# Mixer slots in a new order: gate passes first on VectorE, small multiplies moved to ScalarE

## The reference

```python
proj = jnp.einsum('bsd,ed->bse', x, in_proj_w)
gate = proj[..., :INTER]
hBC  = proj[..., INTER:INTER + CONV_DIM]
...
hBC = jax.nn.silu(conv(hBC) + conv_b)        # depthwise, 4 taps along the sequence
hs, Bm, Cm = ...                             # 128 heads of 64, 8 groups of 128
xch = (hs * dt[..., None])
Y_diag = jnp.einsum('bzlhn,bzshn,bhzls,bzshp->bzlhp', Cc, Bc, L, xch)
states = jnp.einsum('bzlhn,bhzl,bzlhp->bzhpn', Bc, decay_states, xch)
...
Y_off = jnp.einsum('bzlhn,bzhpn,bhzl->bzlhp', Cc, prev, jnp.exp(A_cum))
Y = (Y_diag + Y_off) + hs * D
g = y * jax.nn.silu(gate)
var = jnp.mean(gg * gg, axis=-1, keepdims=True)   # within a group
out = gg * jax.lax.rsqrt(var + EPS) * norm_w
return jnp.einsum('bsi,oi->bso', out, out_proj_w)
```

## Time and profile before

| | us |
|---|---|
| median of 3 runs | 2931.42 (2930.26 to 2935.69) |
| profiled execution | 2935.76 |
| span of the profiled execution | 2934.0 |
| mixer within the span | about 2,070 |

### The profile page before, as it was taken

The page is one execution under the profiler, slowest core; times in us unless marked ns, Lnnn a source line. Parts: engine busy times, 40 slices in busy tenths (PEclk is TensorE's granted clock), DMA queues, the critical chain, the costliest instruction groups (busy, mean ns, idle before and its releaser), DMA issues. The chain is left out here.

```text
span 2934.0 us, 40765 instructions
## 1 busy us (share of the span) xinstructions
PE 2590.2 (88%) x14016; PEld 1766.8 (60%) x14016; DVE 2150.2 (73%) x3375; ACT 1275.0 (43%) x2537; POOL 621.1 (21%) x520
## 2 busy tenths in 40 slices
PE   3579989989999898998999899899698889999899
PEld 2456666666666666666666667665485444444388
DVE  5478888888788878878878888887554646777364
ACT  2344545454453544544445444543222236666421
POOL 2122222212213222221321312223211011110031
PEclk7789999999999999999999999999798889999999
DMA  2322222223222222221322222211102401111000
GB/s 105 78 56 62 61 75 66 54 55 86 56 68 71 64 57 78 66 53 53 87 59 63 75 59 63 79 45 30 76 0 83 165 28 39 39 39 33 1 11 18
DMA packets 194992, 172.58 MB, mean 59 GB/s; under 512 B 31264, under 2 KB 157296, under 8 KB 193136
## 3 DMA queue, kind: packets, MB, share of 16 engines
q1 hardware_dynamic: 189344, 168.13, 20.5%
q10 hardware_dynamic: 5456, 2.00, 0.3%
HBM read 151.70 MB, written 18.38 MB: 58 GB/s over the span
## 5 line engine op out<-in xcount | busy, mean ns | idle before, releaser
L490 PE MATMUL bank<-xh,wh 128*128 128x512 f32 x1152 | 478.9, 416 | 110.7 <-DVE G L824 61.4
L624 PE MATMUL bank<-wo,yt 128*128 128x512 f32 x1024 | 468.1, 611 | 3.8 <-DVE yt L879 2.1
L490 PE MATMUL bank<-xh,wl 128*128 128x512 f32 x1152 | 458.7, 398 | 0.0
L490 PE MATMUL bank<-xl,wh 128*128 128x512 f32 x1152 | 456.5, 396 | 0.0
L790 DVE SCALAR_TENSOR_TENSOR cacc<-raw,cwh,cacc 128x512 f32<-128x512 f32 x480 | 398.7, 831 | 11.3
L624 PEld LDWEIGHTS bank<-wo,yt 128*128 128x128 f32 x1024 | 200.2, 198 | 232.4 <-issue 229.0
L490 PEld LDWEIGHTS bank<-xh,wh 128*128 128x128 f32 x1152 | 220.1, 191 | 165.2 <-DVE G L824 70.1
L698 ACT COPY xs<-bank 128x512 f32<-128x512 f32 x128 | 75.1, 587 | 449.9 <-PE bank L516 449.9
L674 ACT ACTIVATE cth<-cacc 128x512 f32<-128x512 f32 x160 | 102.2, 639 | 346.7 <-DVE cacc L790 346.5
L490 PEld LDWEIGHTS bank<-xh,wl 128*128 128x128 f32 x1152 | 220.3, 191 | 50.3
L490 PEld LDWEIGHTS bank<-xl,wh 128*128 128x128 f32 x1152 | 221.1, 192 | 40.3
(11 more groups left out here) (248 smaller groups left out, 4951.4 us busy)
## 6 DMA issues: line engine op xcount, KB each, us to landing
xn<-w_hs_dram SPq DMA_DIRECT2D x112, 256.0 KB, 2.7
EC<-ecum_scratch SPq DMA_DIRECT2D x112, 256.0 KB, 8.3
xn<-w_gate_dram SPq DMA_DIRECT2D x80, 256.0 KB, 3.0
wo<-w_out_dram SPq DMA_DIRECT2D x8, 2048.0 KB, 8.2
rawx<-w_gate_dram SPq DMA_DIRECT2D x48, 256.0 KB, 3.0
rawx<-w_hs_dram SPq DMA_DIRECT2D x48, 256.0 KB, 2.7
qk_scratch<-at_part SPq DMA_DIRECT2D x48, 256.0 KB
at_qT<-qk_scratch SPq DMA_DIRECT2D x32, 192.0 KB, 2.6
```

The source lines that it names most:

```text
L490: mm = nc.tensor.matmul(BA[bank][:, :], w[:, s, k, :], x[:, k, tok], start=(k == 0 and m == 0), stop=(k == KC - 1 and m == 2))
L624: mm = nc.tensor.matmul(BA[b][:, :], yt[:, j * P:(j + 1) * P], wo[:, j, :], start=(j == 0), stop=(j == JT - 1))
```

## The change

- **xdt**: the two copies `xs` and the multiply on VectorE are replaced by 16 ScalarE activations of 128x64 (`ac_xdt`), each a head's columns straight from PSUM times a scale per partition.
- **Skip and weighing**: hd goes from GpSimd to 8 ScalarE activations of 128x128 at the end of the slot (`ac_skip`); weighing `wo` goes from GpSimd to 8 activations of 128x512 in z0, two at a time between the tile copies (`ac_weigh`).
- **Squares**: the reduction on VectorE is replaced by two halving additions (`dv_fold`) and two accumulating matmuls (`pe_squares`), which stand before the last convolution tile where there is one, and behind the output otherwise.
- **TensorE**: pre, hidden0 and the first diff pair come right behind yoff, ahead of ydiag; hidden1 right behind ydiag (where there are no convolution tiles: behind the second diff pair); the state update and the second diff pair behind both gate tiles.
- **VectorE**: the small copies ahead of the residual; both gate passes (G and `wl`) ahead of the left-over tile's taps; its SiLU behind the state sum; masked decays and folds between that and the new tiles.
- **SyncE**: the rows for the slot after next are loaded behind the gate tiles' loads; the decays apart from them.

```diff
@@ pe_slot
+            if not last:
+                pe_pre(pe, *nxt)
+                pe_hidden(pe, *nxt, 0)
+                pe_diff(pe, *nxt, (0, 1))
-            dv_xc.wait(pe, n + 1)
+            ac_xc.wait(pe, 2 * n + 2)
...
+            if not last and mine:
+                pe_hidden(pe, *nxt, 1)
+            if step:
+                for u in range(2):
+                    release_a(pe, g, z, u)
+                    pe_tile(pe, step, "gate", 2 * (z % CH) + u, bank())
+            if z < NT - 1:
                 po_xd.wait(pe, skip_last(g, z, 1) + 1)
...
+            if not last:
+                pe_diff(pe, *nxt, (2, 3))
+                if not mine:
+                    pe_hidden(pe, *nxt, 1)
...
+            for r in range(len(mine)):
+                if r == len(mine) - 1:
+                    pe_squares(pe, g, z, last)
+                tile(r)
@@ new on ScalarE
+        def ac_xdt(act, g, z, u):
+            n = 8 * g + z
+            h, c = z // CH, z % CH
             pe_hs.wait(act, 2 * n + u + 1)
...
+            for i in range(HG // 2):
+                hh = u * (HG // 2) + i
+                o = nc.scalar.activation(xch[:, hh * HP:(hh + 1) * HP], BT[1 - u][:, i * HP:(i + 1) * HP], ACT.Copy,
+                                         scale=pk[:, h, c, O_DT + hh:O_DT + hh + 1])
+            o.then_inc(ac_xc.sem, 1)
...
+            for j in range(JT):
+                o = nc.scalar.activation(hd[:, j * P:(j + 1) * P], act2[:, h, j, c * P:(c + 1) * P], ACT.Copy,
+                                         scale=Ds[:, h, j:j + 1])
...
+            for j in (2 * i, 2 * i + 1):
+                o = nc.scalar.activation(wo[:, j, :], wo[:, j, :], ACT.Copy, scale=nw[:, 0, j:j + 1])
@@ ac_slot
+            if not last:
+                ac_xdt(act, *nxt, 0)
+                if mine:
+                    ac_xdt(act, *nxt, 1)
+            if step:
+                ac_gate_tanh(act, step, 2 * (z % CH), bank())
+            if not last:
+                ac_relu(act, *nxt, 0)
+                ac_relu(act, *nxt, 1)
+            if step:
+                ac_gate_tanh(act, step, 2 * (z % CH) + 1, bank())
...
@@ dv_slot
+            if step:
+                dv_gate_tile(dve, step, 2 * (z % CH), bank(), n + 1)
+                dv_gate_tile(dve, step, 2 * (z % CH) + 1, bank(), n + 1)
+            for p, i in left:
+                dv_conv_tile(dve, p, i)
...
+            for p, i in left:
                 dv_silu_tile(dve, p, i)
...
+            if not last:
+                dv_masked(dve, *nxt, (0,))
+            dv_fold(dve, n, 0)
+            if not last:
+                dv_masked(dve, *nxt, (1,))
+            dv_fold(dve, n, 1)
...
-            nc.vector.tensor_reduce(sqs[:, :], sq.rearrange("p (j t) -> p t j", j=JT), AX, ALU.add).then_inc(dv_sq.sem, 1)
@@ po_weigh, po_pre
-            nc.gpsimd.tensor_tensor(wo[:, :, :], wo[:, :, :], nw[:, 0, :].unsqueeze(2).broadcast_to([P, JT, C]),
-                                    ALU.mult).then_inc(wo_set, 1)
...
-            nc.gpsimd.tensor_tensor(hd[:, :].rearrange("p (j t) -> p j t", j=JT), act2[:, h, 0:JT, c * P:(c + 1) * P],
-                                    Ds[:, h, :].unsqueeze(2).broadcast_to([P, JT, P]),
-                                    ALU.mult).then_inc(po_hd.sem, 1)
```

More of the change, by code:

```diff
@@ L530, in pe_diff, with pe_squares @@
                 mm.then_inc(pe_df.sem, 1)
+        def pe_squares(pe, g, z, last):
+            n = 8 * g + z
+            dv_sq.wait(pe, 2 * n + 2)
+            if not last:
+                ac_xc.wait(pe, 2 * n + 3)
+            for j in range(2):
+                mm = nc.tensor.matmul(BT[1][:, 0:1], sq[:, j, :], ones1[:, :], start=(j == 0), stop=(j == 1))
+            mm.then_inc(pe_ss.sem, 1)
         def pe_slot(pe, g, z, tiles, bank, last):
@@ L701, in ac_exps, with ac_relu @@
+        def ac_relu(act, g, z, q):
             n = 8 * g + z
             pe_yd.wait(act, 2 * n)
[L703 to L708, removed]
+            pe_df.wait(act, 4 * n + q + 1)
+            nc.scalar.activation(em[:, q, :], BD[q % 2][:, :], ACT.Relu, scale=-1.0).then_inc(ac_mn.sem, 1)
@@ L710, in ac_slot, with ac_exp @@
+        def ac_exp(act, g, z, q):
+            n = 8 * g + z
+            ac_mn.wait(act, 4 * n + q + 1)
+            nc.scalar.activation(em[:, q, :], em[:, q, :], ACT.Exp, scale=-1.0).then_inc(ac_ex.sem, 1)
         def ac_slot(act, g, z, tiles, bank, last):
             n = 8 * g + z
-            h = z // CH
             nxt = (g, z + 1) if z < NT - 1 else (g + 1, 0)
             step, mine = tiles
[L715 to L724, removed]
+            left = left_over(g, z)
@@ L865, in dv_slot @@
                         .then_inc(dv_yo.sem, 1)
+            if not last:
+                dv_small(dve, *nxt)
+            if z > 0:
                 dv_residual(dve, g, z - 1, OUT_BANK[z - 1])
@@ L901, in dv_slot @@
-            for u in range(2):
-                if step:
-                    dv_gate_tile(dve, step, 2 * (z % CH) + u, bank(), n + 1)
-                if not mine and u == 0:
-                    state()
-                    if not last:
-                        dv_small(dve, *nxt)
-            if mine:
-                state()
-            elif not last:
-                dv_xdt(dve, *nxt)
+            left = left_over(g, z)
+            if step:
+                dv_gate_tile(dve, step, 2 * (z % CH), bank(), n + 1)
+                dv_gate_tile(dve, step, 2 * (z % CH) + 1, bank(), n + 1)
@@ L913, in conv @@
+            for p, i in left:
+                dv_silu_tile(dve, p, i)
+            if not last:
+                dv_masked(dve, *nxt, (0,))
+            dv_fold(dve, n, 0)
+            if not last:
+                dv_masked(dve, *nxt, (1,))
+            dv_fold(dve, n, 1)
             def conv(r):
+                if r < len(mine) - 1:
+                    dv_conv_tile(dve, step, mine[r])
                 if r < len(mine):
```

235 lines of the change are left out of this document (107 added, 128 removed).

## The result

The changed kernel takes **2982.94 us** (median of 4 runs, 2980.1 to 2983.63) against 2933.56 in the same comparison: 1.0167 times the kernel before, with a 95% interval of 1.0150 to 1.0185. Forecast were 2926 us and a range of 2894 to 2958.

| slot | before | forecast | after | all slots of the kind, us |
|---|---|---|---|---|
| z1 | 31.37 | 30.0 | 32.59 | +9.8 |
| z2 | 31.61 | 30.0 | 31.41 | -1.6 |
| z5 | 31.21 | 30.0 | 32.80 | +11.1 |
| z6 | 31.71 | 30.0 | 29.58 | -14.9 |
| z0 | 34.25 | 37.0 | 37.79 | +24.8 |

What follows compares the result with a forecast made beforehand. TensorE was taken to bound the mixer, waiting 60.0 us for the gate product and 37.0 for the squares' reduction. Terms -49.5 - 1 + 17.6 + 28.2 - 3.6 + 3 = -5 gave 2926 us, range 2894 to 2958.

Steps and rivals of the forecast that it cites:

- The three-tile slots, -49.5 us forecast: Slots z1, z2, z5, z6: 30.0 us against 31.65 in each of 30 slots, -49.5 us in all.
- the sentence on GpSimd: Three-tile slots: GpSimd's work shrinks and with it the stretching of VectorE's operations, which was not counted.
- the hand schedule: Three-tile slot laid out from its first matmul: TensorE waits 0.5 us before the squares, slot length 30.0 us.
- the 31.65 us of before: Length taken for a three-tile slot of the kernel before, the mean of 31.6 and 31.7 us.
- the long pauses: TensorE's waits in z0, z3 and z7: low clock behind each was charged at 1.25 to 1.5 us.
- z0, +2.2 each forecast: z0: TensorE waits 5.3 us for ScalarE's last weighing of wo; 37.0 us against 34.8, 8 slots, +17.6 us.
- z3 and z7, +28.2 forecast together: hidden1 waits 3.9 and 5.1 us for the left-over SiLU; 26.5 against 24.9, 26.0 against 23.8 us.
- ScalarE's overrun: Rival, chance 0.24: xdt activations above 0.255 us each delay the second gate tanh and VectorE's chain; +24, 2950 us.
- The estimate of 0.24 us: ScalarE, one 128x64 xdt activation by the skill's pointer cost and overlap; the 16 take 3.8 us, just inside.
- the one on the clock: Rival, chance 0.08: 23 longer pauses in z0, z3, z7 each give 0.7 more of low clock; +16, 2942 us.
- the end of the G wait: TensorE's 60.0 us wait for VectorE's gate product goes, as gate passes no longer queue behind taps and xdt product.

Runs made afterwards that it cites:

- e1: The changed kernel with two buffers for xd, so that GpSimd forms xd right behind xdt and not behind the state matmuls: 2910.14 us.
- e5: Control: the changed kernel with two xd buffers, but GpSimd still waits for the state matmuls before forming xd: 2982.32 us.
- e8: The changed kernel with the left-over tile's taps ahead of both gate passes, its tanh and SiLU ahead of the second, in every slot: 2793.20 us.
- e2: The changed kernel with the matmuls of the squares behind the output in every slot, nothing else moved: 2981.87 us.
- e6: The changed kernel with the weighing of wo put back on GpSimd as one operation, started when wo has landed: 2947.70 us.
- e7: The changed kernel with two xd buffers, the left-over tile first in z3 and z7, and z0's output waiting for wo pair by pair: 2756.46 us.

## Why the prediction was wrong

**The three-tile slots, -49.5 us forecast, +4.4 measured.** The step that failed is the sentence on GpSimd: that its work "shrinks, and with it the stretching of VectorE's operations, which I do not count". In sum it did shrink, from 621.1 to 385.9 us. But xd stayed, and the change moved both it and the taps, so that they met. I laid out TensorE, VectorE and ScalarE by the clock and left GpSimd out, although its xd is released by the state matmuls, whose end I had at 13.1 and the taps at 13.4 to 15.7. The taps took 3.90 us by the starts instead of 2.24, and the squares wait was 2.2 instead of 0.5 us in 23 slots. With e1 and e5 this is shown. The trace of before held the warning: its left-over taps took 3.56 us beside hd, and I took the 2.24 of a new tile's. Where GpSimd had no xd (z6), the hand schedule gave 30.0 and the trace 29.58. Of the miss of 54 us, the stretched taps make 23 x 1.66 = 38 and the low clock of the next paragraph 14 x 1.6 = 22; the slots were otherwise 0.4 us shorter than laid out (-13), and the 31.65 us of before were 0.17 above the mean (+5).

**The clock behind a short pause** was a second missing term, which followed from the first: I charged it to the long pauses alone, and had forecast no pause of 2.2 us. This pause cost 1.6 us more in 7 of 8 z1 and 6 of 7 z5, but in only 1 of 8 z2.

**z0, +2.2 each forecast.** The mechanism was as described; the wait was 5.66 us (5.3 forecast), and the low clock cost 1.8 instead of 1.5 us. The group row has a weighing at 728 ns (two took 1.23 us by their starts), where I took 0.59 each: 4.7 us of ScalarE forecast, 4.9 measured. The sum is +24.8 in seven slots, where eight were to cost 17.6, mostly because I took 34.8 us for the slot before, and the mean was 34.25.

**z3 and z7, +28.2 forecast together.** 26.58 and 26.07 us came against 26.5 and 26.0. The waits were 3.94 and up to 5.2 us, as laid out. The sum is nevertheless +15.5, not +28.2: for the slots before I took 24.9 and 23.8 from one window each, which begin behind the wait for the squares of the slot ahead, and the means from output to output are 25.36 and 25.25. With the means of all kinds (31.48 for a three-tile slot instead of 31.65), my lengths would have given about -9 instead of -5. That these slips nearly cancel is luck.

**ScalarE's overrun, the slower rival with 0.24, did not happen.** 0.20 us for one small activation was the value taken, although the 275 ns that it was worked out from belong to an exp of the attention part and not to a copy. The second gate tanh waited for TensorE (0.61 us in z2), not the other way round. The estimate of 0.24 us by the Trainium skill ("ScalarE: Activation LUTs", "What ACT_TABLE_LOAD costs") was high by a fifth. The advice of 512 elements or more in the Trainium skill ("VectorE: DVE Perf Modes", "The TRN2 errata") is about a latency of operations that read SBUF, while the xdt activations read PSUM; it bore on this rival by analogy at most, and TensorE never waited for these activations. So the sign was lost by a mechanism that was not among the rivals at all; the one on the clock had the right sign, but for the long pauses and with 2942 us too small.

**What the change's own parts are worth.** e8 changes only one part, the place of the left-over tile: its taps are ahead of both gate passes again, as in the kernel before, but its tanh and SiLU come between the two. It is 190 us faster than the changed kernel. The other parts with this order are therefore a gain of 4.9% over the kernel before; the place behind both gate passes turns them into a loss. That its place in z3 and z7 is bad was in the forecast; that it is bad in the three-tile slots as well was not: I had given the end of the G wait to both gate passes no longer queueing "behind the taps and the xdt product", and e8 has no G wait with the taps first. Whether the absent xdt product, hd's move off GpSimd or TensorE's new order ended it was not tested apart.

## What to carry to other kernels

When work moves on one engine, lay out every engine that shares something with it on the same time axis, the little busy ones too: here an operation of 1.9 us on an engine busy 13% of the time cost 72 us through its moment alone. Fill an engine's wait for a neighbour with work that is ready, and put the work that has to wait behind it. Before a wait is moved, ask what else the late work releases: taking away only the first wait (e2) gained nothing.

## What the runs showed of the hardware

VectorE did not share with GpSimd, it stood still for nearly all of the other's operation. In z2, xd (1257.94 to 1259.84) kept its 1.90 us, as all 56 of them in the changed kernel, while the taps grew by 1.66; in e6 a `wl` grew by 6.60 us beside a weighing of 7.02. The reverse stands in z2 of the kernel before: hd began 0.14 us behind VectorE's yt product and took 2.85 us; in z3, at 1259.62, it took 1.90. In e7, an xd that ran from 1315.30 to 1317.20 stretched `wl` (VectorE, second fence) but not the G product, which reads PSUM:

```profile
1315.30 1.90 POOL L1013 TENSOR_TENSOR xd<-xch,pk 128x1024 f32<-128x1024 f32 x1 [4.76 <-issue]
```

```profile
1315.69 0.69 DVE L866 SCALAR_TENSOR_TENSOR G<-sg,bank 128x512 f32<-128x512 f32 x1 [2.09 <-ACT sg L682]
1316.30 1.46 DVE L858 TENSOR_TENSOR wl<-rawx,wh 128x512 fp32r<-128x512 f32 x1
```

The Trainium skill, "SBUF — State Buffer", section "SBUF: two separate sides", says that VectorE operations with two SBUF inputs and GpSimd operations that read SBUF lock a shared pair of ports against each other, and that who starts first holds it for the whole instruction. These rows agree: taps, `wl` and the yt product have two SBUF inputs, G has one. The forecast made no use of this rule.

The same pause of 2.2 us was followed by low clock in 7 of 8 z1 and 6 of 7 z5, and in 1 of 8 z2, judged by their lengths (32.8 us or more against 31.2). What tells them apart was not tested and stays open.
